# A layer of phasor attention and top-1 experts on 8 cores: router tiles in two buffers, two of three sums of an attention tile on POOL, carries turned in pairs

## The chip, the cores and the metric

The kernel runs on 8 cores of one Trainium2 chip, one launch, no exchange between the cores. The time is the device time of the slowest core in microseconds (us). A core has five engines that work side by side, each through its own queue in order: PE (matrix products), DVE (vector), ACT (activation functions and copies), POOL (GpSimd) and SP (DMA issue only). Here POOL issues the weight loads and the gathers, SP the plain loads and stores.

## The reference

With x of 4 x 4096 x 1024 (float32), the layer is

```
xn  = layernorm(x)
x + attention(xn) + experts(xn)

attention: k = xn Wk, v = xn Wv (16 heads x 64), phases exp(i 10 k)
  pos   = real( cumsum_t(v * rot_t) * conj(rot_t) ) / sqrt(t+1)
  assoc = real( cumsum_t(v * conj(phase_{t-1})) * phase_t ) / sqrt(t+1)
  out   = (gate0 * pos + gate1 * assoc) Wo
experts: logits = xn gate_w (1024 x 8), expert = argmax, p = its softmax share
  p * ( gelu(xn w1[e] + b1[e]) w2[e] + b2[e] )      w1 1024 x 4096, w2 4096 x 1024
```

## The kernel before

Each core has 2048 own tokens (half of one sequence). It does the experts and the attention's outputs for these, and for the second half of a sequence it needs the sums of the first half too, so every core first runs the sums of 2048 tokens "xfh" and then its own.

**Front (0 to 131 us).** The 16 own tiles of 128 tokens are normed by DVE (`stats` L337, `norm` L351) and ACT (`rstd` L344, Ln and Exp), written as bfloat16 to DRAM (`rows_own` L361), and turned by PE in float32 (`turn_own` L370, the matmuls at L378). `put_own` (L387) copies what was turned from PSUM to `xn32`, one float32 buffer of 8 x 512 columns, that is four tiles. When four are there, `logits` (L401) multiplies them with `gate_w` in float32 (L406, yb<-xn), ACT takes the sums to `lgT` (L416), and `turn_logits` (L421) turns them back. The loop at L1032 writes this order out: the logits of tiles 0 to 3 stand in the turn of tile 4 and so on, and ACT's copy L416 stands right behind PE's sums, ahead of `put_own` of the next tile. `rotor` (L250, DVE) and `rotor_sines` (L276, ACT) make the rotation tables in turns 4, 8 and 12; their last step waits on DVE at L283. `route` (L488) makes the lists of tokens of an expert (for 12 tiles, then 4), `load_xs` (L833) gathers them, `fh_norm` (L562) norms the first xfh tiles.

**Experts 0 to 6 with attention between (131 to 952 us).** For each of 8 experts, `stage1` (L872, 32 column blocks `ct`, matmuls L880) and `stage2` (L929, 64 steps `kc`, matmuls L935) run over 16 pieces of weights of 1 MB (bfloat16 in SBUF, twice that as float32 in DRAM) in a ring of 6 buffers. `feed` (L308) issues the next piece from POOL (L315) once PE has read the one before in that buffer: two after each eighth `ct`, one after each eighth `kc`. `spread` (L1112) lays attention units between: `unit(s)` (L759) is tile s of 128 features x 512 tokens, s = 0 to 63: ACT's sines of tile s-1 (`sins`), PE's keys and values of tile s (`kv`, L621) with ACT's copies, and DVE's `body(s-1)` with `rneg(s)` (L644) in its middle. For s < 32 the body is `sums` (only totals), for s = 32 to 63 it is `outs` (L707): two products of 1024 columns (L726, L729), six scans (L723), two times `rotate` (L654, four instructions of one column), two weighted products (L742, L744), and three sums (L748, L749, L751), the last of which writes `z`, bfloat16. All of this is DVE's. Units 33 to 64, which carry the 32 `outs`, lie in experts 2 to 6. `NCS` = 3 buffers of sines: ACT's copies of tile s wait for `body_t[s-3]`, the weighted product L744 of three tiles before.

**Expert 7 and the end (952 to 1150 us).** `wo_part` (L782) multiplies z with Wo, `load_x` (L776) loads the rows to add to once `body_t[63]` is there, `fetch_rows` and `add_rows` (L807, L817) gather the experts' results and add them.

`out`'s three last instructions of a tile are

```
L748 q2(0) = q2(0) + q2(LR)                     # halves of the position part, pp
L749 pp[2CH:3CH] = pp[2CH:3CH] + pp[3CH:4CH]    # association part
L751 z[c] = q2(0) + pp[2CH:3CH]                 # bfloat16
```

## Time and profile before

| | us |
|---|---|
| median of 3 runs | 1149.34 (1148.93 to 1155.68) |
| the profiled execution's own time | 1152.25 |
| its span, first to last instruction, core 4 (slowest) | 1150.4 |
| spans of the eight cores | 1135.3 to 1150.4 |
| PE busy | 932.1 (81%) |
| PE weight loads | 611.9 (53%) |
| DVE busy | 756.4 (66%) |
| ACT busy | 598.4 (52%) |
| POOL busy (all of it DMA issue) | 162.6 (14%) |

The rows further down come from this execution, on core 4. Times in them are microseconds from the span's start, unless marked ns. "Idle before" is what an engine waited just before an instruction, and the name behind the arrow is what ended that wait.

### The profile page before, as it was taken

Reading aid. Unit: us, or ns where it says so; the run is one execution under the profiler, and the core shown is the slowest. Engines: PE = TensorE matmul, PEld = TensorE weight load, DVE = VectorE, ACT = ScalarE, POOL = GpSimd, SP = SyncE. Lnnn points to the kernel's source line nnn. Section 1 sums busy time; section 2 is a strip of 40 time slices with the busy share of each in tenths; the row PEclk is TensorE's granted clock in tenths of the full one; section 3 lists DMA queues with packets and bytes.
Section 4 is the critical chain, followed back from the end, with each engine's and each line's share of the span. In section 5 each row is a group of like instructions: output and inputs, shape, how many; then the busy total and the mean of one; then the engine's idle time right before and its main releaser. Section 6 shows DMA issues by size and latency. Waiting matters only on the chain.

```text
span 1150.4 us, 18743 instructions; the slowest of 8 cores (1135.3 to 1150.4 us)
## 1 busy us (share of the span) xinstructions
PE 932.1 (81%) x6221; PEld 611.9 (53%) x6296; DVE 756.4 (66%) x1909; ACT 598.4 (52%) x1014; POOL 162.6 (14%) x184
## 2 busy tenths in 40 slices
...
GB/s 190 228 204 205 203 158 172 163 158 106 164 139 160 181 179 162 159 174 169 159 176 170 169 156 175 173 163 159 159 164 167 158 156 196 210 230 217 203 230 79
DMA packets 123779, 199.69 MB, mean 174 GB/s; under 512 B 4755, under 2 KB 70691, under 8 KB 123680
## 3 DMA queue, kind: packets, MB, share of 16 engines
...
## 4 chain that ended last, share of the span: by engine, by line
PE 33%; DVE 22%; issue 18%; DMA 18%; ACT 7%; POOL 1%; DVEq 1%; SPq 0%; ACTq 0%; POOLq 0%
PE yb L935 10%; DMA yg<-ys,gidx 10%; PE wb L621 9%; PE wb L880 8%; DVE pp L723 6%; DMA ring<-w 5%; PE yb L406 3%; DVE pp L729 2%; DVE pp L726 2%; DVE pp L749 1%; DVE pp L677 1%; DVE m L655 1%; PE wb L582 1%; DVE st L340 1%; DMA resf<-xown 1%
## 5 line engine op out<-in xcount | busy, mean ns | idle before, releaser
L880 PE MATMUL wb<-xsT,ring 128*128 128x288 bf16 x2048 | 275.4, 293 | 32.1 <-DMA ring<-w 14.6
L935 PE MATMUL yb<-hT,ring 128*128 128x288 bf16 x2048 | 283.3, 294 | 18.7 <-ACT yT L950 16.5
L880 PEld LDWEIGHTS wb<-xsT,ring 128*128 128x128 bf16 x2048 | 202.6, 100 | 100.7 <-issue 37.2
L935 PEld LDWEIGHTS yb<-hT,ring 128*128 128x128 bf16 x2048 | 204.0, 100 | 90.5 <-issue 26.7
L315 POOL DMA_DIRECT2D ring<-w x128 | 106.1, 832 | 778.9 <-PE yb L935 381.1
L890 ACT ACTIVATE hT<-wb,cfs 128x288 bf16<-128x288 f32 x256 | 118.5, 501 | 100.9 <-PE wb L880 100.1
L650 ACT ACTIVATE cs<-cs 128x512 f32<-128x512 f32 x64 | 40.3, 630 | 116.4 <-DVE cs L644 115.9
L667 DVE COPY cs<-bnd 128x2 f32<-128x2 f32 x64 | 11.1, 173 | 135.1 <-ACT cs L652 134.1
L621 PE MATMUL wb<-xT,wks 128*128 128x512 bf16 x339 | 87.1, 398 | 12.3 <-ACT hT L890 9.7
L621 PE MATMUL wb<-xT,wvs 128*128 128x512 bf16 x383 | 93.0, 386 | 0.1
L723 DVE TENSOR_TENSOR_SCAN pp<-pp,cpos,one 128x256 f32<-128x256 f32 x128 | 88.9, 736 | 3.8 <-DVE pp L729 0.5
L786 PE MATMUL wb<-wos,z 128*128 128x512 bf16 x243 | 64.8, 406 | 22.3 <-DVE resf L795 19.9
L723 DVE TENSOR_TENSOR_SCAN pp<-pp,cas,one 128x512 f32<-128x512 f32 x64 | 80.4, 1257 | 0.0
L950 ACT ACTIVATE yT<-yb,cfs 128x288 bf16<-128x288 f32 x64 | 26.9, 508 | 102.6 <-PE yb L935 102.6
L820 DVE SCALAR_TENSOR_TENSOR resf<-yg,wtok,resf 128x1024 f32<-128x1024 bf16 x16 | 20.4, 1280 | 69.8 <-DMA yg<-ys,gidx 69.8
L378 PE MATMUL wb<-cfs,xnf 128*128 128x128 f32 x128 | 28.7, 399 | 44.8 <-DVE xnf L353 43.6
L621 PEld LDWEIGHTS wb<-xT,wks 128*128 128x128 bf16 x384 | 38.6, 101 | 49.5 <-issue 16.1
L621 PEld LDWEIGHTS wb<-xT,wvs 128*128 128x128 bf16 x384 | 38.4, 100 | 47.9 <-issue 4.6
L633 ACT ACTIVATE cs<-wb,one 128x512 f32<-128x512 f32 x64 | 43.1, 673 | 31.8 <-PE wb L621 31.8
L890 ACT ACT_TABLE_LOAD x40 | 51.3, 1283 | 9.0 <-PE wb L880 8.4
L786 PEld LDWEIGHTS wb<-wos,z 128*128 128x128 bf16 x256 | 26.2, 103 | 50.6 <-issue 29.1
L795 DVE SCALAR_TENSOR_TENSOR resf<-wb,cfs,resf 128x512 f32<-128x512 f32 x32 | 23.0, 747 | 41.9 <-PE wb L786 34.4
...
## 6 DMA issues: line engine op xcount, KB each, us to landing
ring<-w POOLq DMA_DIRECT2D x128, 1024.0 KB, 22.1
...
resf<-xown SPq DMA_DIRECT2D x16, 512.0 KB, 13.6
...
```

The costliest lines, as they stand in the source:

```text
L315: ring_tok[n] = G.dma(d_ring[k], lambda e: e.dma_start(ap(ring[k], 0, [[8 * CH, P], [b, a], [1, b]]), src), *toks)
L378: f = lambda e, a=a, kt=kt, b=b: e.transpose(b[:, a * P:(a + 1) * P], xnf[s2][:, kt * P:(kt + 1) * P], ident)
L406: f = lambda e, kt=kt: e.matmul(b[0:NE, c], gws[:, kt * NE:(kt + 1) * NE], xn32[:, kt * CH + c.start:kt * CH + c.stop], start=(kt == 0), s ...
L621: fn = lambda e, kt=kt, w_=w_, b=b: e.matmul(b[:], w_[:, kt * DM + j * P:kt * DM + (j + 1) * P], src[:, kt * CH:(kt + 1) * CH], start=(kt ...
L633: S.op(lambda e: e.activation(cs[sl][:, CW + 1:2 * CW], b0[:], AF.Identity, bias=c_magic, scale=PSC), toks[0], free, t_ini)
L650: t = S.op(lambda e: e.activation(b, a, AF.Abs), rneg_t[s])
L723: return V.op(lambda e: e.tensor_tensor_scan(q, q, ap(one, 2, [[8, P], [0, n]]), init, ALU.add, ALU.add), tok)
L786: fn = lambda e, j=j: e.matmul(b[:], z[c][:, j * CH + tt * P:j * CH + (tt + 1) * P], wos[:, j * DM + h * CH:j * DM + (h + 1) * CH], start= ...
L880: fn = lambda e, kt=kt, b=b, a=a, k=k: e.matmul(b[:, 0:CAP], ring[k][:, (kt % 4) * DM + a * P:(kt % 4) * DM + (a + 1) * P], xsT[:, kt * CA ...
L890: h_t[ct] = S.op(lambda e, b=b, ct=ct: e.activation(hT[:, ct * CAP:(ct + 1) * CAP], b[:, 0:CAP], AF.Gelu, bias=cf[:, B1 + e_ * NCT + ct:B1 ...
L935: fn = lambda e, d=d, kc=kc, k=k: e.matmul(yb[d][:, 0:CAP], ring[k][:, (kc % 8) * CH + d * P:(kc % 8) * CH + (d + 1) * P], hT[:, kc * CAP: ...
L950: yT_t[h] = S.op(lambda e, d=d, m=m: e.activation(yT[:, m * CAP:(m + 1) * CAP], yb[d][:, 0:CAP], AF.Identity, bias=cf[:, B2 + e_ * KT + m: ...
```

## The change

1. `xn32` becomes two buffers; the second lies on ring buffers 4 and 5, which are first loaded later. Groups of four tiles alternate. So that the ring isn't loaded too early, the first feeds behind `weigh` wait for the last logits.
2. The logits' copy by ACT (`take_logits`) is split from PE's sums and stands one turn later, and `turn_logits` another turn later. At the end of the front, the sums of tiles 12 to 14 and of 15 follow each other, one copy takes both, and `fh_norm(0, 1)` moves ahead of them.
3. In `outs`, the association part moves from `pp` to two buffers `pa0`, `pa1` by the tile's parity. Its sum (L749 before) and the last sum (L751) go to POOL. DVE's product into `pa` waits for POOL's last sum of two tiles before, its product into `pp` for that of the tile before. The weighted product of the association part moves ahead of the second `rotate` and of the position part's, and the order of the two first products and of the scans is changed.
4. `rotate` works on real and imaginary part as one pair: two instructions of two columns in place of four of one, in `sums` and `outs`, with the signed sines laid out in pairs by two small DVE instructions in place of one.
5. `wide` around three operands returns the same columns as before and changes nothing.

```
-    xn32 = sb("xn32", KT * CH, F32, hT_off)[0]
+    xn32 = [sb("xn32%d" % k, KT * CH, F32, o)[0]
+            for k, o in enumerate((hT_off, ring_off + 8192 * (NRING - 2)))]
...
+    yg_off = at[0]
+    pa = [sb("pa0", 2 * CH, F32, pp_off + 4 * 2 * CH)[0], sb("pa1", 2 * CH, F32, yg_off)[0]]
...
-        if i0 + n in (4, 8, 12):
-            xn32_free[0] = t_l
-        t_c = S.op(lambda e: e.activation(lgT[0:NE, c], b[0:NE, c], AF.Identity),
+        xn32_free[i0 // 4 % 2] = t_l
+        return i0, n, c, t_l
+
+    def take_logits(i0, n, c, t_l):
+        t_c = S.op(lambda e: e.activation(lgT[0:NE, c], yb[3][0:NE, c], AF.Identity),
                    t_l, lgT_free[0])
...
-    def rotate(j, re, im, t):
-        V.op(lambda e: e.tensor_scalar(m2[:, 2:3], im, sa(j), None, ALU.mult), t, t_al2[0])
-        t2 = V.op(lambda e: e.tensor_scalar(m2[:, 3:4], re, nsa(j), None, ALU.mult))
-        V.op(lambda e: e.scalar_tensor_tensor(
-            cpos[:, 2 * j:2 * j + 1], re, ca(j), m2[:, 2:3], ALU.mult, ALU.add), t2)
+    def rotate(j, x, t):
+
+        V.op(lambda e: e.tensor_tensor(m2[:, 2:4], x, sab(j), ALU.mult), t, t_al2[0])
         return V.op(lambda e: e.scalar_tensor_tensor(
-            cpos[:, 2 * j + 1:2 * j + 2], im, ca(j), m2[:, 3:4], ALU.mult, ALU.add))
+            cpos[:, 2 * j:2 * j + 2], x, ca(j), ap(m2, 3, [[4, P], [-1, 2]]),
+            ALU.mult, ALU.add), (V.sem, V.n))
...
-        V.op(lambda e: e.tensor_tensor(
+        t_b = V.op(lambda e: e.tensor_tensor(a3, v3, bind, ALU.mult), t, added.get(s - 2))
+        t_p = V.op(lambda e: e.tensor_tensor(
             ap(pp, 0, [[W, P], [CH, 2], [LR, 2], [1, LR]]), v4,
-            ap(rot, 2 * j * LR, [[KT * 2 * LR, P], [0, 2], [LR, 2], [1, LR]]), ALU.mult), t)
-        t_b = V.op(lambda e: e.tensor_tensor(a3, v3, bind, ALU.mult), t)
+            ap(rot, 2 * j * LR, [[KT * 2 * LR, P], [0, 2], [LR, 2], [1, LR]]), ALU.mult), t,
+            added.get(s - 1))
...
         body_t[s] = t2
+        t_g = G.op(lambda e: e.tensor_tensor(A[:, 0:CH], A[:, 0:CH], A[:, CH:2 * CH], ALU.add), t2)
+        t = rotate(j, ends(1), t0)
+        t1 = V.op(lambda e: e.scalar_tensor_tensor(
+            p3, p3, cf[:, GP + j:GP + j + 1], r3, ALU.mult, ALU.mult), t)
         q2 = lambda off: ap(pp, off, [[W, P], [CH, 2], [1, LR]])
         t1 = V.op(lambda e: e.tensor_tensor(q2(0), q2(0), q2(LR), ALU.add), t1)
-        t2 = V.op(lambda e: e.tensor_tensor(
-            pp[:, 2 * CH:3 * CH], pp[:, 2 * CH:3 * CH], pp[:, 3 * CH:4 * CH], ALU.add), t2)
-        z_t[(c, j)] = V.op(lambda e: e.tensor_tensor(
+        added[s] = z_t[(c, j)] = G.op(lambda e: e.tensor_tensor(
             ap(z[c], j * CH, [[KT * CH, P], [LR, 2], [1, LR]]), q2(0),
-            ap(pp, 2 * CH, [[W, P], [LR, 2], [1, LR]]), ALU.add), t2)
+            ap(A, 0, [[2 * CH, P], [LR, 2], [1, LR]]), ALU.add), t1, t_g)
...
-        if turning:
-            turn_logits(*turning)
-            turning = None
+        if taken:
+            turn_logits(*taken)
+            taken = None
+        if summed:
+            taken = take_logits(*summed)
+            summed = None
         if i - 1 in groups and i < NLT - 1:
-            turning = group(i - 1)
+            summed = group(i - 1)
...
-    turning = group(14)
-    late = group(NLT - 1)
-    turn_logits(*turning)
-    turn_logits(*late)
+    fh_norm(0, 1)
+    group(14)
+    turn_logits(*take_logits(12, 4, slice(0, CH), group(NLT - 1)[3]))
...
-    fh_norm(0, 1)
...
-        feed()
+        feed(lg_t[NLT - 1])
```

Three places of the new order, each of before and of the change. The first is ACT's queue in the front, around the logits of tiles 0 to 3 (mv: `rstd`, xn: `put_own`, xnb: `rows_own`, lgT: the copy of the logits), from the `rstd` of tile 5; before:

```order
L346 ACTIVATE mv<-mv,one 128x1
L348 ACTIVATE mv<-mv 128x1
L416 ACTIVATE lgT<-yb 8x512
L392 ACTIVATE xn_74<-wb 128x4x128 x2
L364 ACTIVATE xnb_81<-xnf_115 128x1024
L346 ACTIVATE mv<-mv,one 128x1
L348 ACTIVATE mv<-mv 128x1
L392 ACTIVATE xn_74<-wb 128x4x128 x2
L364 ACTIVATE xnb_79<-xnf_114 128x1024
L346 ACTIVATE mv<-mv,one 128x1
L348 ACTIVATE mv<-mv 128x1
```

and with the change, from the same `rstd` (tile 5's):

```order
L350 ACTIVATE mv<-mv,one 128x1
L352 ACTIVATE mv<-mv 128x1
L396 ACTIVATE xn_75<-wb 128x4x128 x2
L368 ACTIVATE xnb_82<-xnf_118 128x1024
L350 ACTIVATE mv<-mv,one 128x1
L352 ACTIVATE mv<-mv 128x1
L422 ACTIVATE lgT<-yb 8x512
L396 ACTIVATE xn_75<-wb 128x4x128 x2
L368 ACTIVATE xnb_80<-xnf_117 128x1024
L350 ACTIVATE mv<-mv,one 128x1
L352 ACTIVATE mv<-mv 128x1
```

The copy lgT stood ahead of the next tile's xn; now the xn of tile 4 (in the second buffer, xn_75), a row copy and a `rstd` stand ahead of it.

The second is DVE's queue from the middle of one `outs` tile to its end (m and cpos are `rotate`, cs_48 is `rneg` of the next tile); before, from the first of the second half's scans to the end of the tile:

```order
L723 SCALAR_TENSOR_TENSOR pp<-pp,cpos,one 128x256 x2
L723 SCALAR_TENSOR_TENSOR pp<-pp,cas,one 128x512
L655 TENSOR_SCALAR m_127<-pp,al 128x1
L656 TENSOR_SCALAR m_127<-pp,al 128x1
L657 SCALAR_TENSOR_TENSOR cpos<-pp,al,m_127 128x1
L659 SCALAR_TENSOR_TENSOR cpos<-pp,al,m_127 128x1
L741 COPY cas<-pp 128x2
L742 SCALAR_TENSOR_TENSOR pp<-pp,cfs,rot 128x1024
L744 SCALAR_TENSOR_TENSOR pp<-pp,cfs,cs_47 128x1024
L748 TENSOR_TENSOR pp<-pp 128x2x256
L749 TENSOR_TENSOR pp<-pp 128x512
L751 TENSOR_TENSOR z_87<-pp 128x512
```

and with the change, from the second half's scans to the first products of the tile behind:

```order
L729 SCALAR_TENSOR_TENSOR pa_95<-pa_95,cas,one 128x512
L729 SCALAR_TENSOR_TENSOR pp<-pp,cpos,one 128x256 x2
L748 COPY cas<-pa_95 128x2
L749 SCALAR_TENSOR_TENSOR pa_95<-pa_95,cfs,cs_48 128x1024
L662 TENSOR_TENSOR m_130<-pp,al 128x2
L663 SCALAR_TENSOR_TENSOR cpos<-pp,al,m_130 128x2
L754 SCALAR_TENSOR_TENSOR pp<-pp,cfs,rot 128x1024
L757 TENSOR_TENSOR pp<-pp 128x2x256
L672 COPY cs_46<-bnd 128x2
L673 COPY bnd<-cs_46 128x2
L732 TENSOR_TENSOR pa_96<-vb_49,cs_46 128x1024
L733 TENSOR_TENSOR pp<-vb_49,rot 128x1024
```

Two sums of 512 columns are gone from the end, `rotate` has two instructions, and the association part's weighted product stands before it.

The third is POOL's queue at the end of expert 2 and in `stage1` of expert 3, whose first three attention tiles are among the first of `outs`; before:

```order
L315 DMA ring_72<-w 128x4x1024
L315 DMA ring_67<-w 128x4x1024
L315 DMA ring_68<-w 128x4x1024
L835 DMA xsr<-xr,idx 96x1024 x3
L315 DMA ring_69<-w 128x8x512
L315 DMA ring_70<-w 128x8x512
L315 DMA ring_71<-w 128x8x512
L315 DMA ring_72<-w 128x8x512
L315 DMA ring_67<-w 128x8x512
L315 DMA ring_68<-w 128x8x512
```

and with the change:

```order
L319 DMA ring_72<-w 128x4x1024
L752 TENSOR_TENSOR pa_96<-pa_96 128x512
L758 TENSOR_TENSOR z_87<-pp,pa_96 128x512
L319 DMA ring_67<-w 128x4x1024
L319 DMA ring_68<-w 128x4x1024
L842 DMA xsr<-xr,idx 96x1024 x3
L752 TENSOR_TENSOR pa_95<-pa_95 128x512
L758 TENSOR_TENSOR z_87<-pp,pa_95 128x512
L319 DMA ring_69<-w 128x8x512
L319 DMA ring_70<-w 128x8x512
L752 TENSOR_TENSOR pa_96<-pa_96 128x512
```

The feeds stand now behind the sums of the tile whose unit came before them.

## Rows read from the trace of the kernel before

**Rows 1.** The chain that ended last, its longest pieces, in order: start, us, what

```profile
29.60 8.56 PE yb L406 x16
...
119.85 7.65 DMA xsr<-xr,idx
```

**Rows 2.** Waits of the whole run: us in total, times, longest

```profile
DVE cs L667 <- ACT cs L652: 134.1, 30, 11.8
...
PE wb L880 <- DMA ring<-w: 14.6, 6, 4.3
```

**Rows 3.** Experts 3 to 6: PE, PEld, DVE, ACT, POOL busy, PEclk, DMA share, GB/s

```profile
488.00:599.00 111.00, 96.68 (x703) 67.24 (x708) 98.42 (x181) 64.06 (x106) 16.95 (x19) 0.95 1.10 169
599.00:724.00 125.00, 104.96 (x717) 70.96 (x724) 108.58 (x197) 67.59 (x113) 17.80 (x19) 0.89 1.09 168
724.00:841.00 117.00, 100.45 (x714) 68.31 (x721) 110.72 (x203) 66.89 (x112) 17.63 (x19) 0.93 1.06 162
841.00:952.00 111.00, 94.64 (x665) 64.83 (x671) 105.37 (x192) 61.04 (x104) 17.60 (x20) 0.94 1.09 162
```

**Rows 4.** Timeline of DVE over one tile of `outs` in expert 5

```profile
748.12 0.17 DVE L667 COPY cs<-bnd 128x2 f32<-128x2 f32 x1
...
748.47 1.22 DVE L726 TENSOR_TENSOR pp<-vb,rot 128x1024 f32<-128x1024 bf16 x1
...
753.41 0.18 DVE L655 TENSOR_SCALAR m<-pp,al 128x1 f32<-128x1 f32 x1
...
754.09 0.68 DVE L644 SCALAR_TENSOR_TENSOR cs<-cs 128x512 f32<-128x512 f32 x1
...
761.03 0.68 DVE L749 TENSOR_TENSOR pp<-pp 128x512 f32<-128x512 f32 x1
...
762.42 0.16 DVE L667 COPY cs<-bnd 128x2 f32<-128x2 f32 x1
```

**Rows 5.** L315, the ring's loads issued in 435 to 702, then in 728 to 840

```profile
L315 POOL DMA_DIRECT2D ring<-w x37: 740/873/942, 434.3 to 695.9; - x37
...
DMA to landing us min/median/max: 17.0/28.6/34.0
...
DMA to landing us min/median/max: 10.4/21.0/27.3
```

**Rows 6.** Timeline around the first logits: start, us, engine, line, idle before

```profile
36.99 0.21 DVE L342 BATCH_NORM_AGGREGATE mv<-st 128x2 f32<-128x12 f32 x1
...
38.24 0.59 ACT L416 ACTIVATE lgT<-yb 8x512 f32<-8x512 f32 x1 [8.34 <-PE yb L406]
...
40.63 0.28 ACT L346 ACTIVATE mv<-mv,one 128x1 f32<-128x1 f32 x1
...
41.38 0.81 DVE L353 TENSOR_SCALAR xnf<-xt,mv 128x1024 f32<-128x1024 f32 x1 [4.18 <-ACT mv L348]
```

**Rows 7.** Timeline of turns 12 and 13: the third group, then the sines

```profile
79.70 0.59 ACT L416 ACTIVATE lgT<-yb 8x512 f32<-8x512 f32 x1 [8.14 <-PE yb L406]
...
88.65 0.17 DVE L283 TENSOR_SCALAR al<-al 128x8 f32<-128x8 f32 x1 [17.78 <-ACT al L282]
```

**Rows 8.** Timeline of the end of the front

```profile
108.67 0.28 ACT L346 ACTIVATE mv<-mv,one 128x1 f32<-128x1 f32 x1
...
108.90 0.20 PE L424 MATMUL yb<-cfs,lgT 8*128 8x8 f32 x1 [0.23 <-ACT lgT L416]
...
110.79 0.18 DVE L498 TENSOR_REDUCE rd<-yb 128x4 f32<-128x32 f32 x1
```

**Rows 9.** DMA issues: KB of each, median us from issue to landing

```profile
wvs<-wv POOLq DMA_DIRECT2D x1, 2048.0 KB, 41.1
```

**Rows 10.** Timeline of POOL in expert 5

```profile
736.43 1.48 POOL L315 DMA_DIRECT2D ring<-w  x2 [11.43 <-PE wb L880]
740.64 1.28 POOL L835 DMA_INDIRECT xsr<-xr,idx  x1 [2.74 <-DMA ys<-xsr]
```

**Rows 11.** The chain again, at the end of the attention

```profile
963.25 9.29 DMA resf<-xown
```

More of the change, by code:

```diff
@@ L125, in build_program @@
             for i in range(NRES)]
-    ring = []
-    ring_off = at[0]
+    ring, ring_off = [], at[0]
     for k in range(NRING):
@@ L282, in rotor_sines @@
         t_al = S.op(lambda e: e.activation(col(5), col(2), AF.Sin))
-        t_al2[0] = V.op(lambda e: e.tensor_scalar(col(6), col(5), -1.0, None, ALU.mult), t_al)
+        V.op(lambda e: e.tensor_scalar(
+            ap(al, 6 * KT, [[8 * KT, P], [2, KT]]), col(5), -1.0, None, ALU.mult), t_al)
+        t_al2[0] = V.op(lambda e: e.tensor_copy(
+            ap(al, 6 * KT + 1, [[8 * KT, P], [2, KT]]), col(5)), t_al)
         carry_t[0] = t_al2[0]
@@ L407, in logits @@
                 b[0:NE, c], gws[:, kt * NE:(kt + 1) * NE],
-                xn32[:, kt * CH + c.start:kt * CH + c.stop],
+                xn32[i0 // 4 % 2][:, kt * CH + c.start:kt * CH + c.stop],
                 start=(kt == 0), stop=(kt == KT - 1))
@@ L609, in build_program @@
     sin_t, cos_t, rneg_t, v_t, body_t = {}, {}, {}, {}, {}
-    z_t = {}
+    z_t, added = {}, {}
     t_wkv = [None]
@@ L686, in half @@
                 m2[:, 0:2], m2[:, 0:2], cpos[:, 2 * j:2 * j + 2], ALU.add), tt)
-            carry_t[0] = rotate(j, m2[:, 0:1], m2[:, 1:2], tt)
+            carry_t[0] = rotate(j, m2[:, 0:2], tt)
         def assoc(a):
@@ L711, in outs @@
         W = 4 * CH
+        A = pa[s % 2]
         p3 = ap(pp, 0, [[W, P], [CH, 2], [1, CH]])
@@ L719, in outs, with scan @@
         probe = ap(cs[sl], 1, [[2 * CW, P], [CW, 2], [1, CH]])
-        def scan(off, n, init, tok):
-            q = pp[:, off:off + n]
+        def scan(b, off, n, init, tok):
+            q = b[:, off:off + n]
             return V.op(lambda e: e.tensor_tensor_scan(
                 q, q, ap(one, 2, [[8, P], [0, n]]), init, ALU.add, ALU.add), tok)
-        V.op(lambda e: e.tensor_tensor(
+        t_b = V.op(lambda e: e.tensor_tensor(a3, v3, bind, ALU.mult), t, added.get(s - 2))
+        t_p = V.op(lambda e: e.tensor_tensor(
             ap(pp, 0, [[W, P], [CH, 2], [LR, 2], [1, LR]]), v4,
-            ap(rot, 2 * j * LR, [[KT * 2 * LR, P], [0, 2], [LR, 2], [1, LR]]), ALU.mult), t)
-        t_b = V.op(lambda e: e.tensor_tensor(a3, v3, bind, ALU.mult), t)
+            ap(rot, 2 * j * LR, [[KT * 2 * LR, P], [0, 2], [LR, 2], [1, LR]]), ALU.mult), t,
+            added.get(s - 1))
         re, im = cpos[:, 2 * j:2 * j + 1], cpos[:, 2 * j + 1:2 * j + 2]
-        scan(0, LR, re, t_b)
-        t0 = scan(LR, LR, im, t_b)
-        scan(2 * CH, CH, cas[:, 2 * j:2 * j + 1], t_b)
-        t = rotate(j, pp[:, LR - 1:LR], pp[:, CH - 1:CH], t0)
-        yield
-        scan(CH, LR, re, t)
-        t0 = scan(CH + LR, LR, im, t)
-        t_a = scan(3 * CH, CH, cas[:, 2 * j + 1:2 * j + 2], t_b)
-        t = rotate(j, pp[:, CH + LR - 1:CH + LR], pp[:, 2 * CH - 1:2 * CH], t0)
-        last = ap(pp, 3 * CH - 1, [[W, P], [CH, 2]])
+        ends = lambda h: ap(pp, h * CH + LR - 1, [[W, P], [LR, 2]])
+        scan(pp, 0, LR, re, t_p)
+        t0 = scan(pp, LR, LR, im, t_p)
+        scan(A, 0, CH, cas[:, 2 * j:2 * j + 1], t_b)
+        t = rotate(j, ends(0), t0)
+        yield
+        t_a = scan(A, CH, CH, cas[:, 2 * j + 1:2 * j + 2], t_b)
+        scan(pp, CH, LR, re, t)
+        t0 = scan(pp, CH + LR, LR, im, t)
+        last = ap(A, CH - 1, [[2 * CH, P], [CH, 2]])
         carry_t[0] = V.op(lambda e: e.tensor_copy(cas[:, 2 * j:2 * j + 2], last), t_a)
-        t1 = V.op(lambda e: e.scalar_tensor_tensor(
-            p3, p3, cf[:, GP + j:GP + j + 1], r3, ALU.mult, ALU.mult), t)
         t2 = V.op(lambda e: e.scalar_tensor_tensor(
@@ L870, in build_program @@
     yr_t = {}
+    wide = lambda x: x[:, 0:CAP]
     def stage1(e_, at_ct):
@@ L880, in stage1 @@
                     fn = lambda e, kt=kt, b=b, a=a, k=k: e.matmul(
-                        b[:, 0:CAP],
+                        wide(b),
                         ring[k][:, (kt % 4) * DM + a * P:(kt % 4) * DM + (a + 1) * P],
-                        xsT[:, kt * CAP:(kt + 1) * CAP], start=(kt == 0), stop=(kt == KT - 1))
+                        wide(xsT[:, kt * CAP:(kt + 1) * CAP]), start=(kt == 0), stop=(kt == KT - 1))
                     if a == 7 and kt == 3:
```

23 lines of the change are left out of this document (11 added, 12 removed).

## The prediction

> **What bounds the kernel now.** I read the chain of waits first, then the waits in total, then the stages one by one, since the shares of the page (PE 81%, DVE 66%) are means over stages with different limits.
>
> In the front the chain runs through PE's float32 logits: 8.56 us for the first group of four tiles, and two more pieces of over 8 us like it [rows 1]. From 131 us to about 460 PE is the bound: DVE waits there for ACT's sines, which make 134.1 us in all [rows 2]. From 488 to 952, experts 3 to 6, two things are close to their limit at once [rows 3]. DVE is busy 98 of 111, 109 of 125, 111 of 117 and 105 of 111 us. One `outs` tile starts at 748.12 and the next at 762.42, a pitch of 14.30 us with no hole in it [rows 4]. And the ring is tight: loads issued from 434 to 696 take 28.6 us to land (median), 21.0 later [rows 5], and PE waits 14.6 us for the ring in the whole run [rows 2]. In these four stages the DMA moves 169, 168, 162 and 162 GB/s [rows 3]. The DMA share alone (above 1) says little. So DVE can give up time only until the loads are the limit: if 169 GB/s is what this mix reaches, 162 GB/s over 228 us leaves 228 x 7/169 = 9 us in experts 5 and 6, and what has been loaded ahead by 952 may add some 5 us.
>
> **Front: logits in two buffers, copied later.** Before, ACT waits 8.34 us for the sums at 38.24, then copies, and only at 40.63 reaches the `rstd` whose statistics DVE had finished at 36.99 + 0.21 = 37.20; DVE waited 4.18 us and norms tile 6 at 41.38 [rows 6]. With the change the copy of tile 4 (second buffer), the row copy and this `rstd` stand ahead of the lgT copy. Norm 6 can come at some 38.0. But PE is in the logits until 29.60 + 8.56 = 38.16 as before, tile 5 is turned only then, and ACT has lgT, xn and xnb (40.63 - 38.24 = 2.4 us) ahead of the `rstd` of tile 7. So of the 3.4 us one tile later only 2.4 are left. From there the loop of norm, statistics and `rstd` runs at its own pitch again. Two such groups: 4.8 us.
>
> The third group is worth more. The lgT copy waits 8.14 us at 79.70, and behind it ACT makes the sines for which DVE's queue waits until 88.65 (17.78 us) [rows 7]. The copy now stands behind the sines, so these start right after tile 12 is put, while PE still sums: the 8.1 us and most of its 0.59 go, some 8.3. PE's sums end before the next tile is normed.
>
> At the end the `rstd` of the first xfh tiles stood behind the last logits' copy, at 108.67, and `route(12, 4)` on DVE began at 110.79, behind these norms, though its logits were turned at 108.90 + 0.20 [rows 8]. With the norms first and one larger copy I take 1.3 of these 1.7 us. Sum 4.8 + 8.3 + 1.3 = 14.4 us.
>
> I take off 2.4 us. The loads don't shrink: `wv` took 41.1 us to land [rows 9], and the gather of expert 0's tokens, whose last load takes 7.65 us [rows 1], now follows closer behind it. PE needs the gather before anything else. So 12 us, bounds 7 and 15. From there to 435 the ring has room and the shift is carried along; in the tight stretch both ends of the loop move with it.
>
> **DVE's tile.** Gone: L749 and L751. From 761.03 to the next tile's 762.42 that is 1.39 us [rows 4]. `rotate` from 753.41 to 754.09 is 0.68 us for four instructions; of the two new ones, the second waits for the first, as now L657 for L656, so about 0.42. Twice a tile: 0.52 us. The other order of products and scans changes no count; I set it to 0. Tile: 14.30 - 1.91 = 12.39 us. In the `sums` tiles the 0.52 us lies in DVE's waits for ACT [rows 2]: nothing. The one small instruction more in the front: under 0.2 us.
>
> **What POOL's sums cost DVE.** The trace shows no sum on POOL. Two costs are possible. First the new wait: DVE's product into `pp` waits for POOL's last sum. Ahead of it lie two edge copies and the product into `pa`, 748.47 - 748.12 + 1.22 = 1.57 us [rows 4], so a sum of up to some 1.4 us is hidden. Behind that product stands the whole tile. Second, POOL's sum may hold up DVE's instructions that read SBUF twice, which is nearly all of them. Bounds: 0; and POOL's slowest row, 1.28 us [rows 10], each time, 2.56 us a tile. The nearest row for a sum of 512 columns is DVE's own L749, 0.68 us [rows 4]. I take that: 1.37 a tile come back, and the tile is 12.39 + 1.37 = 13.76 us, 0.54 less than before.
>
> Over 24 tiles of experts 4 to 6 that is 13 us (expert 3, at 169 GB/s, is limited by its loads). I count 6, since the loads leave 9 to 14 and the ring is fed later, which comes next. Bounds -14 and +16.
>
> The Trainium skill ("SBUF — State Buffer", Who interferes with whom) speaks against the change: DVE and GpSimd share one pair of ports, and a DVE instruction with two SBUF inputs and a GpSimd one that reads SBUF exclude each other for the whole instruction. "GPSIMD Engine Reference" (3.1) has 4497 ns for a float32 sum of 2048 columns, estimated 1.1 us for 512; then 2.2 us a tile come back and nothing is left. No run yet shows it.
>
> **The feeds.** On POOL every feed now stands behind the sums of the tile before it. In expert 5 a feed went out at 736.43, as PE released it [rows 10]; the body that now goes ahead of it ended on DVE at 748.12 [rows 4]. The loads go out up to 12 us later, with 21 us to land. Where PE comes to wait, its next unit comes later too, and DVE's lag behind PE, which makes those 12 us, shrinks. I count it within the 6 us above.
>
> **The tail.** `load_x` waits for `body_t[63]`, the product L744, and the chain waits 9.29 us for that load from 963.25 [rows 11]. L744 now stands ahead of `rotate` (0.42) and L742 (1024 columns like L726, 1.2): 1.6 us earlier. PE's last products need POOL's last sum only for tiles 12 to 15.
>
> **Sum.** 12 + 6 + 1.6 = 19.6 us. The profiled execution took 1152.25 us (span 1150.4), so 1132.6; the median of the runs stands 2.9 us below it, 1149.3 - 19.6 = 1129.7. Forecast 1130, its own range 1124 to 1138.
>
> **Rivals.**
> A, POOL's sums shut DVE out for their full length. With 1.28 us each [rows 10], the tile is 12.39 + 2.56 = 14.95 us, 0.65 more than before; 24 tiles add 16 us, against 13.6 from front and tail: 1151. For it: nearly every DVE instruction of the tile has two inputs in SBUF. Against: no row. 0.3. This is the mechanism of the rule named above; by the page's price it would be 12.39 + 2.2 = 14.6 us a tile and 1143.
> B, the sums cost DVE nothing. The tile is 12.39 us, 46 us less over 24 tiles; the loads stop that at 14. 12 + 14 + 1.6 = 27.6: 1122. For it: POOL is busy 17 of 111 us a stage [rows 3]. 0.2.
> C, the other side: late feeds starve PE. Three pairs of buffers go round. PE needs 94.64/8 = 11.8 us for two pieces and a unit [rows 3]. With a feed waiting 12 us and 28.6 us to land [rows 5], three tiles take 52.4 us, 17.5 each, as long as DVE's lag doesn't shrink; with 21.0 us to land it is 14.9. At 15.4 the 32 tiles lose 1.1 us each, 35 us, less 13.6: 1171. It decides as soon as feed wait and landing exceed 3 x 14.3 - 11.8 = 31.1 us. Against it: PE waiting means a shorter lag. 0.12.
> D, the front gives nothing, since its loads set its end; then the forecast is 1142. For it: `wv`'s 41.1 us [rows 9]. Against: PE and ACT, not loads, end the waits of the chain there [rows 1]. 0.05; the forecast itself has 0.33.
>
> **Range and chances.** 1% is about what a measurement of this kernel tells from no change, 11.5 us. Forecast (0.33) and B (0.2) lie below 1137.8, with some 0.07 of A's chance, where a sum costs near 0.9 us: 0.6 in all. Within 1%: the rest of A, D, and a mild C, 0.29. Slower: C, 0.11. The range for 8 of 10 goes from 1115 to 1155: it holds forecast, B, A, D and leaves most of C out.
>
> **What would show it.** Right: the first L880 at 117 to 121 us where it was at 131.1; a DVE tile pitch of 13.5 to 14; the feed rows of POOL waiting for DVE; no hole in DVE ahead of the product into `pp`. A would show as DVE rows lengthened (1.22 or 1.28 to over 2 us) beside POOL's sums and a pitch of 14.6 or more. B: rows as before and a pitch near 12.4, with PE waiting for the ring. C: PE's wait for the ring far over 14.6 us, above all at L880, and DVE waiting for ACT's sines inside experts 4 to 6. D: turns done earlier, but a long wait for the gather before the first turned tokens. The forecast is wrong if time changes elsewhere, as in expert 7, of which I expect the same length.

## The result and the profile after

| | before | after |
|---|---|---|
| median of four runs each, us | 1152.51 (1148.93 to 1155.76) | 1206.18 (1205.30 to 1209.64) |
| ratio, with its interval | | 1.0472 (1.0425 to 1.0519) |
| span of the profiled core | 1150.4 | 1204.6 |
| first matmul of expert 0 / 3 / 7 | 131.1 / 488.4 / 951.8 | 130.9 / 481.4 / 991.9 |

The change makes the kernel 4.7% slower, where 1.7% faster was forecast. Here and below a median is over all runs of a kernel, a ratio over those outside the slower state that this program shows at times, so that the two can differ a little. By the last row experts 0 to 2 take 350.6 us in place of 357.2 (7 less), experts 3 to 6 take 510.5 us in place of 463.4 (47 more), and expert 7 with the end takes 212.7 in place of 198.6 (14 more). That is 54 us, the difference of the spans.

Experts 3 to 6 after the change, in windows (the columns of [rows 3]):

```profile
481.00:607.00 126.00, 100.40 (x707) 68.49 (x706) 96.77 (x135) 63.88 (x105) 34.84 (x33) 0.91 0.98 150
607.00:736.00 129.00, 102.13 (x726) 68.70 (x724) 115.94 (x160) 68.67 (x115) 37.63 (x36) 0.92 0.93 143
736.00:870.00 134.00, 106.30 (x722) 70.33 (x721) 111.34 (x152) 67.31 (x111) 36.27 (x35) 0.88 0.89 139
870.00:992.00 122.00, 99.10 (x672) 66.60 (x671) 101.56 (x139) 60.07 (x101) 32.22 (x31) 0.89 0.91 146
```

Against [rows 3] the stages are 47 us longer, while DVE's busy time hardly moves (426 us in place of 423) and PE's grows by 11 (408 in place of 397, at a mean granted clock of 0.90 in place of 0.93; whether that clock fell by the waits or beside them isn't shown). POOL's is twice what it was, and the loads, at 162 to 169 GB/s before, fall to 139 to 150. No engine is busy all the time, and the loads are slower than they were: the engines wait for each other. The waits in total (us, times, longest), against [rows 2]:

```profile
POOL pa L752 <- DVE m L662: 303.1, 32, 24.1
...
DVE cs L672 <- ACT cs L658: 167.4, 32, 15.8
...
PE wb L889 <- DMA ring<-w: 67.1, 18, 10.1
...
DVE pp L733 <- POOL z L758: 1.2, 1, 1.2
```

PE waits 67.1 us for the ring where it waited 14.6, and POOL stands 303.1 us at the first sum of a tile with the feeds behind it. The wait that DVE was given for POOL's last sum costs 1.2 us in the whole run.

**DVE's tile.** Timeline of DVE over one full tile of `outs` in expert 5 (start, us), with the start of the next; [rows 4] is its counterpart:

```profile
767.67 0.16 DVE L672 COPY cs<-bnd 128x2 f32<-128x2 f32 x1
...
768.01 2.30 DVE L732 TENSOR_TENSOR pa<-vb,cs 128x1024 f32<-128x1024 bf16 x1
...
774.30 0.22 DVE L663 SCALAR_TENSOR_TENSOR cpos<-pp,al,m 128x2 f32<-128x2 f32 x1
...
779.22 1.26 DVE L663 SCALAR_TENSOR_TENSOR cpos<-pp,al,m 128x2 f32<-128x2 f32 x1
...
782.59 0.16 DVE L672 COPY cs<-bnd 128x2 f32<-128x2 f32 x1
```

The pitch is 14.92 us. Two rows are stretched: the product L732 from 1.22 to 2.30, and the second of two equal instructions L663 from 0.22 to 1.26. That is where POOL's two sums stand, as its own timeline shows:

```profile
709.34 0.90 POOL L319 DMA_DIRECT2D ring<-w  x1
...
723.02 1.27 POOL L758 TENSOR_TENSOR z<-pp,pa 128x512 bf16<-128x512 f32 x1 [2.41 <-DVE pp L757]
724.23 3.75 POOL L319 DMA_DIRECT2D ring<-w  x5
...
739.44 0.77 POOL L319 DMA_DIRECT2D ring<-w  x1
764.28 1.26 POOL L752 TENSOR_TENSOR pa<-pa 128x512 f32<-128x512 f32 x1 [24.08 <-DVE m L662]
767.95 1.27 POOL L758 TENSOR_TENSOR z<-pp,pa 128x512 bf16<-128x512 f32 x1 [2.41 <-DVE cs L672]
769.17 1.51 POOL L319 DMA_DIRECT2D ring<-w  x2
...
779.20 1.27 POOL L752 TENSOR_TENSOR pa<-pa 128x512 f32<-128x512 f32 x1 [4.28 <-DVE m L662]
```

POOL starts its last sum at 767.95, DVE's product L732 at 768.01, and the product ends 1.08 us late. POOL's first sum of the tile starts at 779.20, DVE's L663 at 779.22, and that one ends 1.04 us late. The same rows show the feeds. None goes out between 710.24 and 724.23, then five in one clump; and none between 740.21 and 769.17, since the sum ahead of them waits 24.08 us. PE over that seam between experts 4 and 5:

```profile
735.83 1.12 PE L889 MATMUL wb<-xsT,ring 128*128 128x288 bf16 x4 [6.75 <-DMA ring<-w]
742.79 4.35 PE L889 MATMUL wb<-xsT,ring 128*128 128x288 bf16 x20 [5.85 <-DMA ring<-w]
```

and DVE at the first unit behind it:

```profile
753.84 0.17 DVE L672 COPY cs<-bnd 128x2 f32<-128x2 f32 x1 [15.81 <-ACT cs L658]
```

So it is a loop: a late feed stops PE, PE's next unit comes late, DVE has no work for 15.81 us, POOL's sum stands behind that, and with it the next feed.

**The chain.** Its longest pieces (start, us, what), against [rows 1]:

```profile
107.87 19.35 DMA xsr<-xr,idx
...
726.47 30.63 DMA ring<-w
...
992.83 29.27 DMA wos<-wo
```

Before, one long DMA stood in the front (7.65 us). Now it is 19.35 us. Loads of the ring make 12.8% of the chain where they made 5.0%: before, long ones stood at the starts of experts 3 and 4 alone, now at those of experts 3 to 6. And `wo`, issued at 931.24 before, is issued only at 992.83, behind the start of expert 7, where PE waits 16.7 us for it.

**The front.** Its timeline at the places of [rows 6 to 8], all engines:

```profile
73.92 0.17 DVE L285 TENSOR_SCALAR al<-al 128x8 f32<-128x8 f32 x1 [9.06 <-ACT al L284]
...
95.32 0.19 DVE L504 TENSOR_REDUCE rd<-yb 128x4 f32<-128x32 f32 x1 [0.19 <-PE yb L430]
...
127.46 2.08 PE L858 MATMUL wb<-cbs,xsr 96*128 96x96 bf16 x24 [17.63 <-DMA xsr<-xr,idx]
```

Tile 6 is normed at 37.88 (41.38 before), the sines end at 73.92 (88.65), `route(12, 4)` begins at 95.32 (110.79), 15.5 us earlier, and the last gather is issued at 107.87, 12 us earlier. Then PE waits 17.63 us for it, and expert 0 begins 0.3 us earlier than before. `wv` explains it: issued at 76.93, it takes 48.3 us to land (41.1 in [rows 9]), until 125.2, and the last gather, issued behind it from the same queue, lands at 127.2. The runs x6_loads, x8_both and x10_spread below test this.

### The profile page after: what moved, and what is told of

Its sections match the earlier page's. It is cut to its first block, busy times and chain, and to the rows that moved or that the text cites. A ratio compares the mean times of both kernels' runs of the same rounds, so it can differ in the third digit from the quotient of the medians.

```text
span 1204.6 us, 18654 instructions; the slowest of 8 cores (1188.3 to 1204.6 us)
## 1 busy us (share of the span) xinstructions
PE 944.2 (78%) x6296; PEld 612.1 (51%) x6296; DVE 740.5 (61%) x1590; ACT 598.3 (50%) x1013; POOL 240.1 (20%) x248
## 4 chain that ended last, share of the span: by engine, by line
DMA 27%; DVE 26%; PE 24%; issue 13%; ACT 7%; POOL 1%; DVEq 1%; SPq 0%; ACTq 0%; POOLq 0%
DMA ring<-w 13%; DMA yg<-ys,gidx 9%; PE wb L889 9%; PE wb L627 6%; PE yb L944 6%; DVE pp L729 4%; DVE cpos L663 2%; DMA wos<-wo 2%; DVE pa L729 2%; DVE pp L754 2%; DVE pa L749 2%; DVE pp L733 2%; DVE pa L732 2%; DMA xsr<-xr,idx 2%; DVE st L344 1%
## 5 line engine op out<-in xcount | busy, mean ns | idle before, releaser
L889 PE MATMUL wb<-xsT,ring 128*128 128x288 bf16 x2048 | 282.1, 297 | 83.0 <-DMA ring<-w 67.1
L944 PE MATMUL yb<-hT,ring 128*128 128x288 bf16 x2048 | 287.8, 297 | 29.5 <-ACT yT L959 18.3
L627 PE MATMUL wb<-xT,wks 128*128 128x512 bf16 x384 | 96.6, 397 | 7.3 <-ACT hT L899 7.3
L752 POOL TENSOR_TENSOR pa<-pa 128x512 f32<-128x512 f32 x32 | 40.3, 1260 | 303.1 <-DVE m L662 303.1
L793 PE MATMUL wb<-wos,z 128*128 128x512 bf16 x256 | 67.3, 410 | 37.1 <-DVE resf L802 20.4
L729 DVE TENSOR_TENSOR_SCAN pa<-pa,cas,one 128x512 f32<-128x512 f32 x64 | 81.2, 1268 | 0.0
L732 DVE TENSOR_TENSOR pa<-vb,cs 128x1024 f32<-128x1024 bf16 x32 | 60.6, 1893 | 0.0
```

Source lines behind the costliest of these rows:

```text
L627: fn = lambda e, kt=kt, w_=w_, b=b: e.matmul(b[:], w_[:, kt * DM + j * P:kt * DM + (j + 1) * P], src[:, kt * CH:(kt + 1) * CH], start=(kt ...
L729: return V.op(lambda e: e.tensor_tensor_scan(q, q, ap(one, 2, [[8, P], [0, n]]), init, ALU.add, ALU.add), tok)
L732: t_b = V.op(lambda e: e.tensor_tensor(a3, v3, bind, ALU.mult), t, added.get(s - 2))
L752: t_g = G.op(lambda e: e.tensor_tensor(A[:, 0:CH], A[:, 0:CH], A[:, CH:2 * CH], ALU.add), t2)
L793: fn = lambda e, j=j: e.matmul(b[:], z[c][:, j * CH + tt * P:j * CH + (tt + 1) * P], wos[:, j * DM + h * CH:j * DM + (h + 1) * CH], start= ...
L889: fn = lambda e, kt=kt, b=b, a=a, k=k: e.matmul(wide(b), ring[k][:, (kt % 4) * DM + a * P:(kt % 4) * DM + (a + 1) * P], wide(xsT[:, kt * C ...
```

## The experiments

Ratios are to the kernel before on the same chip; its median was 1142.66 us for x1 to x4, 1144.75 for x5 to x8 and 1143.22 for x9 and x10. The expectations of x1 to x4 are in us of the first chip, where the kernel before took 1152.5: to compare them with what was measured, go by the ratio.

### x1_front, x2_dve: the front alone; all but POOL's sums

x1_front keeps points 1, 2 and 5 of the change, with the old `rotate` and `outs`. x2_dve is the changed kernel with both sums back on DVE:

```
-        t_g = G.op(lambda e: e.tensor_tensor(A[:, 0:CH], A[:, 0:CH], A[:, CH:2 * CH], ALU.add), t2)
...
-        added[s] = z_t[(c, j)] = G.op(lambda e: e.tensor_tensor(
+        t_g = V.op(lambda e: e.tensor_tensor(A[:, 0:CH], A[:, 0:CH], A[:, CH:2 * CH], ALU.add), t2)
+        added[s] = z_t[(c, j)] = V.op(lambda e: e.tensor_tensor(
...
```

> The front's part of the change alone (two float32 buffers, logits copied later, norms moved ahead); rotate and the outs tiles as before. In the changed kernel's trace the tokens' gather was issued 12 us earlier but landed at the same time, behind the load of wv, and by expert 3 it stood 7 us ahead of the kernel before. Theory 1 (the loss lies in the outs tiles, the front is nearly neutral): 1144 to 1152 us. Theory 2 (the front itself disturbs the order of the loads and costs part of the loss): over 1158 us.

> The changed kernel, but the two sums of an attention tile are on DVE again (pairs in rotate, second buffer and new order are kept). The DVE tile should be 14.3 - 0.52 = 13.8 us. Theory 1 (POOL's sums cause the whole loss, by whatever way): 1138 to 1148 us. Theory 2 (the new order of products and scans, or rotate in pairs, costs something itself): a tile pitch over 14.3 us and 1155 us or more.

Measured: x1_front 1141.26 us, 0.9983 (0.9957 to 1.0008); the last gather takes 20.86 us and expert 0 begins at 128.9. x2_dve 1128.91 us, 0.9892 (0.9870 to 0.9915). Both fall into the range of their theory 1 (as ratios 0.993 to 1.000 and 0.987 to 0.996). What follows: the front is worth next to nothing, as rival D had it, and the two sums on POOL turn a gain of 1.1% into a loss of 4.7%. In x2_dve L732 is back at 1219 ns (mean) and PE waits 9.9 us for the ring.

### x3_tiny: the same waits and order, without the work

```
-        t_g = G.op(lambda e: e.tensor_tensor(A[:, 0:CH], A[:, 0:CH], A[:, CH:2 * CH], ALU.add), t2)
+        t_g = G.op(lambda e: e.tensor_tensor(A[:, 0:1], A[:, 0:1], A[:, CH:CH + 1], ALU.add), t2)
...
-            ap(z[c], j * CH, [[KT * CH, P], [LR, 2], [1, LR]]), q2(0),
-            ap(A, 0, [[2 * CH, P], [LR, 2], [1, LR]]), ALU.add), t1, t_g)
+            z[c][:, j * CH:j * CH + 1], pp[:, 0:1], A[:, 0:1], ALU.add), t1, t_g, t_0)
```

> The changed kernel with POOL's two sums cut to one column each (the sums are left out, so z is zero but for one column), with all their waits and their places in POOL's queue. It keeps the feeds behind each tile's body but takes away the time in which POOL's sums could shut DVE out. Theory 1 (late feeds starve PE): still 1165 to 1200 us, PE's wait for the ring far above 14.6 us. Theory 2 (DVE shut out by the sums is the cause): 1120 to 1135 us, with a DVE tile of 12.4 us and no long waits for the ring.

In the first four tiles, POOL also clears z with a memset of 3.5 us each. Measured: 1152.93 us, 1.0092 (1.0065 to 1.0118), just below the range of theory 1 (1.011 to 1.041) and far from that of theory 2. The tile is 12.8 us, and still PE starves:

```profile
POOL pa L755 <- DVE m L662: 284.8, 32, 22.6
...
PE wb L891 <- DMA ring<-w: 44.9, 14, 5.9
```

So the place of the sums in POOL's queue alone, with 0.18 and 0.25 us of work, eats all that a DVE tile shorter by 1.5 us would give, and more. It is a cause of its own, but not the whole.

### x4_free: the work without the waits

```
-        t_g = G.op(lambda e: e.tensor_tensor(A[:, 0:CH], A[:, 0:CH], A[:, CH:2 * CH], ALU.add), t2)
+        G.op(lambda e: e.tensor_tensor(z[c][:, j * CH:(j + 1) * CH], cf[:, 0:CH], cf[:, 128:128 + CH], ALU.add), t_set)
```

and the last sum likewise, of constants that lie ready.

> The changed kernel with two full sums of 512 float32 columns on POOL per tile, but of constants, so that they wait for nothing of their tile and hold up no feed (the real two sums are left out). DVE still meets POOL's sums. Theory 1 (late feeds are the loss, the shut-out only eats DVE's saving): 1130 to 1150 us, POOL's feeds waiting for PE again. Theory 2 (the shut-out is the loss): 1185 us or more, DVE rows lengthened by about 1 us twice a tile.

Measured: 1164.59 us, 1.0250 (1.0166 to 1.0334), between what the two theories expected, and nearer to theory 2 (1.028 or more). The interval is wide by one run of four, 1180.22; the others have 1163.5 to 1165.2. PE waits only 1.9 us for the ring here, so this loss is the shut-out. It falls wherever a sum happens to stand. Means of DVE's groups over the whole run (busy us, mean ns):

```profile
L733 DVE TENSOR_TENSOR pp<-vb,rot 128x1024 f32<-128x1024 bf16 x32 | 52.0, 1626 | 0.0
...
L757 DVE TENSOR_TENSOR pp<-pp 128x512 f32<-128x512 f32 x32 | 28.3, 885 | 3.4
```

L733 had 1214 ns in the changed kernel, L757 692. Two pairs of sums on POOL and a later one, and what DVE did beside the two pairs:

```profile
742.64 1.28 POOL L752 TENSOR_TENSOR z<-cfs 128x512 bf16<-128x512 f32 x1
744.07 1.26 POOL L758 TENSOR_TENSOR z<-cfs 128x512 bf16<-128x512 f32 x1
...
747.15 1.31 POOL L752 TENSOR_TENSOR z<-cfs 128x512 bf16<-128x512 f32 x1
748.61 1.54 POOL L758 TENSOR_TENSOR z<-cfs 128x512 bf16<-128x512 f32 x1
...
765.85 2.08 POOL L758 TENSOR_TENSOR z<-cfs 128x512 bf16<-128x512 f32 x1
```

```profile
744.06 2.36 DVE L754 SCALAR_TENSOR_TENSOR pp<-pp,cfs,rot 128x1024 f32<-128x1024 f32 x1
746.52 2.50 DVE L757 TENSOR_TENSOR pp<-pp 128x512 f32<-128x512 f32 x1
748.95 1.23 DVE L672 COPY cs<-bnd 128x2 f32<-128x2 f32 x1
```

L754 takes 1.29 elsewhere, L757 0.69, the copy of two columns 0.16: each meets a sum of its own (744.07, 747.15, 748.61) and is longer by 1.07, 1.81 and 1.07 us. It works the other way too, POOL's sum at 765.85 takes 2.08 us beside DVE. In expert 5 DVE is busy 115.7 us here and 97.7 in x3_tiny, 2.25 us for each of its eight tiles, so each sum costs DVE 1.1 us. x4_free is slower than x5_behind below, and again by DVE: in experts 3 to 6 DVE is busy 447.6 us here and 431.7 there, and the stages take 487.9 and 473.0 us. Where the sums fall decides their price: the tiles are uneven (12.8 to 17.9 us).

### x5_behind, x9_tiny_behind: the sums queued behind the feeds

x5_behind is the changed kernel with POOL's sums of a tile issued one unit later, behind the feeds; x9_tiny_behind does the same to x3_tiny:

```
+        def pool_sums():
+            t_g = G.op(lambda e: e.tensor_tensor(A[:, 0:CH], A[:, 0:CH], A[:, CH:2 * CH], ALU.add), t2)
...
+        held.append(pool_sums)
...
     def unit(s):
+        while held:
+            held.pop(0)()
```

> The changed kernel, but POOL's two sums of a tile are put into its queue one unit later, so that the feeds between two units go out ahead of them. The real sums stay on POOL, with the same waits of DVE for them. Theory 1 (two costs that add: feeds late, and DVE shut out during the sums): the feeds' part goes and the shut-out stays, a tile pitch of about 14.9 us, PE's wait for the ring near 15 us, ratio to before 1.00 to 1.02. Theory 2 (the shut-out alone explains the loss once real data is waited for): over 1.035.

> The fourth corner of a table of two causes: POOL's sums cut to one column (both sums left out, as in x3_tiny) and put behind the feeds (as in x5_behind). So far, as ratios to before: both causes 1.047, feeds late alone 1.009, shut-out alone 1.006. Theory 1 (two causes that reinforce each other, since the loop of feeds, loads and DVE is as long as its slowest part allows): 0.975 to 0.985, that is each cause alone costs about 0.03 and together 0.07. Theory 2 (the loads limit these stages whatever DVE takes, so that a shorter tile gains nothing more): no better than x2_dve, 0.987 or more, though its tile is 12.8 us.

Measured: x5_behind 1151.44 us, 1.0057 (1.0033 to 1.0081). DVE's tile is as long as in the changed kernel, but the ring is fed:

```profile
PE wb L898 <- DMA ring<-w: 15.0, 11, 2.8
```

```profile
754.38 2.30 DVE L732 TENSOR_TENSOR pa<-vb,cs 128x1024 f32<-128x1024 bf16 x1
...
769.27 2.30 DVE L732 TENSOR_TENSOR pa<-vb,cs 128x1024 f32<-128x1024 bf16 x1
```

The pitch is 14.89 us. x9_tiny_behind: 1123.16 us, 0.9832 (0.9796 to 0.9869), a tile of 12.8 us. Its window over expert 3 (expert 5 has 170 GB/s):

```profile
479.00:585.00 106.00, 95.54 (x713) 66.56 (x710) 86.70 (x137) 64.26 (x107) 31.84 (x36) 0.98 1.11 172
```

x5_behind and x9_tiny_behind both fall into the range of their theory 1. With this the two causes stand in a table of four kernels:

| ratio to before | POOL's full sums (DVE shut out) | sums of one column |
|---|---|---|
| ahead of the feeds | 1.047 (the change) | 1.009 (x3_tiny) |
| behind the feeds | 1.006 (x5_behind) | 0.983 (x9_tiny_behind) |

The shut-out alone costs 0.023, late feeds alone 0.026, both together 0.064: they feed each other, by some 0.015 (the intervals are 0.002 to 0.005 to either side, some 0.007 for the 0.015). That x9_tiny_behind beats x2_dve by only 0.6%, though its tile is 1.4 us shorter, fits a limit by the loads: they move 167 to 173 GB/s in experts 3 to 6, PE waits 25.8 us for the ring, and in expert 7 it waits 15.7 us for `wo`. No run with faster loads tests it. If it is so, a part of the 0.015 is this floor under the fourth kernel. In both kernels with sums of one column z is nearly all zero; what that does to PE's last products isn't taken apart.

### x7_order: the old order of products and scans

x2_dve with the old `outs`, the paired `rotate` kept (a tile's end):

```
+        t1 = V.op(lambda e: e.scalar_tensor_tensor(
+            p3, p3, cf[:, GP + j:GP + j + 1], r3, ALU.mult, ALU.mult), t)
         t2 = V.op(lambda e: e.scalar_tensor_tensor(
             a3, a3, cf[:, GA + j:GA + j + 1], probe, ALU.mult, ALU.mult), carry_t[0])
         body_t[s] = t2
-        t = rotate(j, ends(1), t0)
-        t1 = V.op(lambda e: e.scalar_tensor_tensor(
-            p3, p3, cf[:, GP + j:GP + j + 1], r3, ALU.mult, ALU.mult), t)
```

> Front and pairs in rotate as in the changed kernel, but the outs tile otherwise as before: one buffer, the old order of products and scans, all sums on DVE. In x2_dve the tile took 14.17 us where I expected 13.8. Theory 1 (the new order costs 0.4 us a tile in short holes between dependent instructions, the pairs save 0.52): a tile of 13.8 us, ratio 0.980 to 0.989. Theory 2 (rotate in pairs saves less than worked out): 14.1 to 14.2 us and the ratio of x2_dve or a little above.

Measured: 1128.52 us, 0.9844 (0.9786 to 0.9901), a pitch of 13.71 us where x2_dve has 14.18. The tile and the ratio are as theory 1 had them. In x2_dve the end of a tile reads

```profile
756.59 0.22 DVE L663 SCALAR_TENSOR_TENSOR cpos<-pp,al,m 128x2 f32<-128x2 f32 x1
756.91 1.28 DVE L753 SCALAR_TENSOR_TENSOR pp<-pp,cfs,rot 128x1024 f32<-128x1024 f32 x1
758.30 0.69 DVE L756 TENSOR_TENSOR pp<-pp 128x512 f32<-128x512 f32 x1
```

and in x7_order

```profile
756.33 0.22 DVE L663 SCALAR_TENSOR_TENSOR cpos<-pp,al,m 128x2 f32<-128x2 f32 x1
756.47 0.16 DVE L747 COPY cas<-pp 128x2 f32<-128x2 f32 x1
...
757.85 1.28 DVE L750 SCALAR_TENSOR_TENSOR pp<-pp,cfs,cs 128x1024 f32<-128x1024 f32 x1
759.05 0.68 DVE L754 TENSOR_TENSOR pp<-pp 128x512 f32<-128x512 f32 x1
```

The same kinds of instructions, but where one has to wait for the one just before it, the starts lie 0.32 and 1.39 us apart; where it doesn't, 0.14 and 1.20. The new order has more such neighbours, 0.47 us a tile in all. The intervals of x7_order and x2_dve overlap, so what this gives in the whole time isn't shown.

x7_order differs from x1_front in the paired `rotate` and its table alone, so these two runs price point 4 of the change by itself: 0.9983 (0.9957 to 1.0008) without the pairs, 0.9844 (0.9786 to 0.9901) with them. The pairs are worth some 1.4% (0.8 to 2.0), where the front is worth 0.2. Not all of it comes from the `outs` tiles. First matmul of expert 0 and of expert 2, and the time between them (us):

| | expert 0 | expert 2 | experts 0 and 1 |
|---|---|---|---|
| before | 131.13 | 384.28 | 253.15 |
| x1_front (new front, old `rotate`) | 128.92 | 383.08 | 254.16 |
| x7_order (new front, pairs) | 130.13 | 376.37 | 246.24 |
| after | 130.85 | 377.35 | 246.50 |

On all eight cores the time between the two is 251.0 to 254.2 us in the two kernels with the old `rotate` and 244.9 to 247.3 in the two with pairs. These experts hold only `sums` tiles. Where DVE has no hole, such a tile takes 6.35 us with the old `rotate` and 5.74 with the pairs. And the chain of the kernel before runs there, at times, through `rotate` (L655, L657) and on to the statistics of the next norm (L340), for which ACT waits:

```profile
183.85 0.21 DVE m L655
...
184.30 0.17 DVE cpos L657
...
188.89 0.69 DVE st L340
```

### x6_loads, x8_both, x10_spread: the front's loads moved

x6_loads is x2_dve with `wk` and `wv` issued at turns 4 and 7 and two pieces of the ring held back until behind the gather; x8_both does that to x7_order; x10_spread keeps the pieces at turns 1 and 4 and issues `wk` at turn 7, `wv` at turn 9:

```
-        if i in (1, 4, 7, 9):
+        if i in (1, 4):
             feed(loaded[-1][1])
-        if i == 11:
+        if i == 7:
             G.dma(d_wkv, lambda e: e.dma_start(w3(wks), wsrc(wk)), loaded[-1][1])
+        if i == 9:
+            t_wkv[0] = G.dma(d_wkv, lambda e: e.dma_start(w3(wvs), wsrc(wv)), loaded[-1][1])
...
-    for _ in range(NRING - 4):
+    for _ in range(NRING - 2):
         feed(lg_t[NLT - 1])
```

> The changed kernel with all three sums on DVE (as in x2_dve), and the loads of the front in another order: wk and wv take the places of the ring's third and second-last early pieces, and these two pieces go out behind the tokens' gather. Theory 1 (the front's end is set by the loads queued ahead of the gather): the gather lands 8 to 12 us after its issue in place of 20, the first L889 comes at 115 to 121 us in place of 128, and the ratio falls by 0.006 to 0.011 below that of x2_dve (0.989). Theory 2 (the gather takes 20 us whatever stands ahead of it, by its own descriptors): the same time as x2_dve.

> x7_order with the loads of x6_loads: the version that should beat both kernels. If both theories 1 hold, the ratio is 0.970 to 0.982; if neither, 0.989.

> x8_both with the same two ring pieces behind the gather, but wk and wv issued later (turns 7 and 9 in place of 4 and 7) and the second ring piece earlier. In x8_both the gather is issued 5 us later than in x2_dve, since the loads of x tiles stand behind wk and wv. If a later wv lets the x tiles through, the gather is issued at 102 to 105 us and the first L888 comes at 116 to 120: ratio 0.970 to 0.976. If what counts is only how many bytes go ahead of the gather, it lands when it did: 0.976.

Measured: x6_loads 1126.78 us, 0.9796 (0.9720 to 0.9872), expert 0 from 121.8; x8_both 1118.13 us, 0.9758 (0.9701 to 0.9815), expert 0 from 120.9; x10_spread 1112.70 us, 0.9722 (0.9690 to 0.9754), expert 0 from 117.7. PE's wait for the gather in x10_spread:

```profile
114.28 2.08 PE L857 MATMUL wb<-cbs,xsr 96*128 96x96 bf16 x24 [3.60 <-DMA xsr<-xr,idx]
```

PE's wait is 17.60 us in x7_order, 2.40 in x8_both, 3.60 in x10_spread. The last gather lands 21.4 us after its issue in x7_order and 8.3 us after it in x10_spread: the 13 us that the reordered front makes were there all along, behind the loads. From x7_order to x10_spread the ratio falls by 0.012, and the intervals are apart. Of the loads in front of the gather, the early ring pieces had landed by 82.67 in the changed kernel, `wk` at 105.96 and `wv` at 125.2, so it is these two that stood in the way, `wv` above all. The kernel before had only 2.43 us of this wait, so with its own front it had no more than that to gain from the loads; no run tests that. The three ratios lie where they were expected, that of x10_spread in the first of its two cases. The intervals of x8_both and x10_spread overlap; x10_spread has the lowest time of this study and beats both before and after.

## Why the prediction was wrong, step by step

**Front, 14.4 us less 2.4 for the loads.** The walk through the engines was right: norm of tile 13 14.7 us earlier (13.1 in the sum), `route(12, 4)` 15.5 (14.4). The deduction failed. "The gather ... now follows closer behind it" was priced at 2.4 us, and at expert 0 it cost all but 0.3. Rival D, given 0.05, is what happened; I argued against it from what ended the chain's waits before the change, which says nothing of what stands second. What had to be worked out is the landing after the move: `wv`, issued 2.5 us earlier at 76.93, lands at 118.0 by [rows 9], and 7.65 us for the last gather behind it [rows 1] make 125.7, only 1.8 us before the 127.5 of the kernel before (the 76.93 was read afterwards; before, `wv` went out at 79.42).

A sentence of the Trainium skill bears on this: by "DMA: Bandwidth & Descriptors" (Two DMAs through the same engine are not ordered), descriptors within one queue of a DMA engine start in order, while the end of a later one doesn't tell that an earlier one has written. The trace fits both: the three gathers, issued 28 us and more behind `wv`, land only at 123.2, 124.8 and 127.2, and the first two of them ahead of its 125.2.

**The pairs in the `sums` tiles, "nothing".** The 0.52 us was said to lie in DVE's waits for ACT there. That DVE waits there shows only that it has time at the end of a tile; `rotate` stands in its queue ahead of `rneg` and of the statistics of a norm, and the chain ran through it. The term measured 7 us, nearly all that the changed kernel has won by expert 3: experts 0 and 1 take 246.5 us in place of 253.2, and 254.2 in x1_front, which has the new front and the old `rotate`. The forecast didn't have this gain; had it not come, the forecast would have been further off.

**DVE's tile, 1.91 us shorter.** The pairs save 0.59 us (14.30 to 13.71 in x7_order; 0.52 forecast), the two sums 1.4. "The other order of products and scans changes no count; I set it to 0" was wrong by 0.47: counts were the same, neighbours were not. 12.39 + 0.47 is 12.86, and x3_tiny and x9_tiny_behind have 12.8.

**What POOL's sums cost DVE, taken as 1.37 a tile.** The new wait was hidden, as worked out (1.2 us in all). The second cost was mis-sized: 14.9 - 12.8 = 2.1 us. I took DVE's own time for a sum, 0.68, as the nearest row; a POOL sum takes 1.26 or 1.27 us and holds a DVE instruction for nearly all of that. Rival A's 14.95 us was the tile that came. By itself it makes 1.006, where the prediction had 1151 us for A (1.0015).

The page "SBUF — State Buffer" (Who interferes with whom) of the Trainium skill, which the prediction weighed and gave 0.3, was right in this case, in both directions: 0.22 to 1.26 us on DVE, 1.26 to 2.08 on POOL. The 1.1 us that the prediction estimated for POOL's sum from the page "GPSIMD Engine Reference" (3.1) of the Trainium skill measured 1.26.

**The feeds, "within the 6 us above".** This failed most. I wrote that DVE's lag shrinks where PE waits. It does, but POOL's sum then waits for a unit that PE has not begun (24.08 us), so feeds come later, not earlier. Rival C, given 0.12, named the mechanism, its rows (PE's wait far over 14.6 us, DVE waiting for ACT's sines inside the experts) and the side. Its condition, feed wait plus landing over 31.1 us, was worked out for evenly spaced feeds with a landing of 28.6. In the changed kernel a load takes 15.0 us (median in 480 to 990), 27 with a wait of 12, so for an even tile that test would have said no; what bites is the seam between experts, where held feeds leave in a clump, and the fourth of five lands 30.63 us after its issue, the fifth 37.4. C expected 1171. Alone it makes 1.009 (x3_tiny), together with A 1.047.

**Mid part and tail.** In x5_behind, with the same tile of 14.9 us, experts 3 to 6 take 473.0 us, 10 more than before, or 13 with the 0.7% between the chips; so some 34 to 37 of their 47 us are the feeds', with what the two causes do to each other. Expert 7, of which the same length was expected, takes 14 us more with `wo` on the chain; in x5_behind it is 198.8 us, as before. So this, too, was the feeds.

**Rivals as if exclusive.** A, C and D all came true. I had summed each against the forecast of the other terms, and the range's upper end, 1155, left out every pair of them. A and C in particular share a cause, DVE's lag, and should have been priced together.

**Loads as a floor.** The 9 to 14 us left to experts 3 to 6 was too little: x9_tiny_behind passes them in 434.7 us, against 463.4 before (chips differ by 0.8%, some 4 us of it). The loads move 167 to 173 GB/s there in place of 162 to 169. Rate times length is 74.2 MB in place of 76.7, so the rest of the bytes has been moved outside of these stages, and a part of the gain is handed back: expert 7 and the end take 205.2 us in place of 198.6.
